# Window mixing on one core: 64-row transposes in two banks, and normalisation moved to GpSimd

## The reference, cut to what matters

```
x = x + mixing(groupnorm(x), w, b)        # 16 heads of 16 channels, windows of 8 x 8 cells
x = x + attention(groupnorm(x), ...)      # projections, depthwise conv, linear attention

def mixing(x, w, b):                      # w: [16, 64, 64], b: [16, 64]
    pad by 4 on every side, cut into 9 x 9 windows of 64 cells
    y[n, head, i, d] = sum_j w[head, i, j] * xw[n, head, j, d] + b[head, i]
    put the windows back, cut the padding off
```

## Time and profile before

| | |
|---|---|
| Median of 3 runs | 2488.25 us (2484.59 to 2489.66) |
| The profiled execution | 2490.49 us, of which its span is 2488.8 us |
| Busy share of the span | PE 95%, PEld 76%, DVE 80%, ACT 60%, POOL 44% |
| Mixing stage, first and last records | image load at 0.8 us, last add to the image at 259.3 us |

### The profile page before, as it was taken

One profiled execution on the slowest core, in us unless ns is written; L12 is line 12 of the kernel. 1 busy time (PEld: TensorE's weight loads), 2 busy tenths in 40 slices (PEclk: granted clock), 3 DMA queues, 4 the chain that ended last, 5 costly groups with the idle time before them and its releaser, 6 DMA issues. The chain is left out here.

```text
span 2488.8 us, 66780 instructions
## 1 busy us (share of the span) xinstructions
PE 2364.8 (95%) x25485; PEld 1886.2 (76%) x25485; DVE 1992.4 (80%) x2652; ACT 1495.8 (60%) x1864; POOL 1099.0 (44%) x1477
## 2 busy tenths in 40 slices
PE   5999799999999999799999999999999889999998
PEld 5889687777787788577888888888888656666666
DVE  7887588787688786788888888888888578888775
ACT  5777576665566566566677677667767433443342
POOL 6722387787787787300000000000000068888887
PEclk9999899999999999899999999999999999999999
DMA  7874688988889889988888888888888677777774
GB/s 283 342 293 177 212 301 313 325 294 306 307 281 323 320 282 321 267 204 204 206 213 208 208 208 210 207 207 212 210 206 209 215 251 271 279 278 271 270 271 135
DMA packets 300877, 628.38 MB, mean 252 GB/s; under 512 B 50688, under 2 KB 252160, under 8 KB 291456
## 3 DMA queue, kind: packets, MB, share of 16 engines
q1 hardware_dynamic: 295616, 590.90, 77.1%
q10 hardware_dynamic: 4048, 31.11, 3.5%
q0 software_dynamic: 1008, 3.67, 0.4%
HBM read 327.81 MB, written 300.94 MB: 253 GB/s over the span
## 5 line engine op out<-in xcount | busy, mean ns | idle before, releaser
L1901 POOL TENSOR_TENSOR ql<-image,qh 128x1024 fp32r<-128x1024 f32 x128 | 305.3, 2410 | 971.4 <-ACT qh L1929 971.4
L1555 PE MATMUL c_ps<-dh,wh 128*128 128x512 f32 x1152 | 463.5, 402 | 17.5 <-DVE wl L1706 13.1
L1470 ACT ACTIVATE dh<-image 128x1632 fp32r<-128x1632 f32 x192 | 301.5, 1570 | 266.7 <-PE c_ps L1555 250.6
L1555 PE MATMUL c_ps<-dh,wl 128*128 128x512 f32 x1152 | 455.0, 395 | 0.0
L1555 PE MATMUL c_ps<-dl,wh 128*128 128x512 f32 x1152 | 453.6, 394 | 1.3 <-issue 1.3
L1664 DVE TENSOR_TENSOR dl<-image,dh 128x1632 fp32r<-128x1632 f32 x192 | 356.4, 1856 | 72.2 <-ACT dh L1470 72.2
L1125 PE MATMUL o_ps<-xh,wqh 128*128 128x512 f32 x768 | 320.8, 418 | 11.0 <-issue 7.6
L1125 PE MATMUL o_ps<-xl,wqh 128*128 128x512 f32 x768 | 304.6, 397 | 0.0
L1125 PE MATMUL o_ps<-xh,wql 128*128 128x512 f32 x768 | 303.4, 395 | 0.0
L1555 PEld LDWEIGHTS c_ps<-dh,wh 128*128 128x128 f32 x1152 | 217.7, 189 | 70.1 <-DVE wl L1706 13.2
L1555 PEld LDWEIGHTS c_ps<-dl,wh 128*128 128x128 f32 x1152 | 217.3, 189 | 53.4 <-issue 1.3
(11 more groups left out here) (210 smaller groups left out, 5024.0 us busy)
## 6 DMA issues: line engine op xcount, KB each, us to landing
qkv_scratch<-stage SPq DMA_DIRECT2D x384, 408.0 KB, 4.0
image<-qkv_scratch SPq DMA_DIRECT2D x189, 816.0 KB, 6.3
qr_scratch<-qs SPq DMA_DIRECT2D x128, 256.0 KB, 3.0
yq_scratch<-qy SPq DMA_DIRECT2D x64, 512.0 KB, 6.7
image<-qr_scratch SPq DMA_DIRECT2D x128, 256.0 KB, 6.2
image<-yq_scratch SPq DMA_DIRECT2D x128, 256.0 KB, 5.9
ox<-x_scratch SPq DMA_DIRECT2D x8, 4096.0 KB, 14.8
out<-ox SPq DMA_DIRECT2D x7, 4096.0 KB, 12.7
```

The costliest lines, as they stand in the source:

```text
L1470: act.activation(dh[kind][:, :], raw[kind], ACT.Copy).then_inc(hi_ready, 1)
L1555: last = pe.matmul(c_ps[:, m, :], w[hp][:, kind, part, o:o + P], cells[:, :, HALF * dy:HALF * dy + HALF * NB], start=(k == 0), stop=(k == 5))
L1901: pool.tensor_tensor(two_of(ql, n, tp), two(n, tp), two_of(qh, n, tp).bitcast(F32), ALU.subtract)\
```

## The change

Five things are edited.

1. A turn has 16 transposes in place of 8: each takes 64 partitions (one array tile of 64 rows and 128 columns) with the 64 x 64 corner of the identity moving through it. The two row halves `ch` alternate, and each has a bank of the pair to itself. `xT` is laid out accordingly as [half of the channels of a tile, window pair and ct, 64 channels].
2. Turning back likewise has 16 transposes of 64 rows; the half v goes to bank v of the pair, and the cells are written in image order.
3. `add_back` adds a bank at a time, 2 operations of 512 elements for even n, and 448, 64, 448, 64 for odd n, in place of 1,024, and 768, 128, 128.
4. The exchange of window rows of tile ct = 1 moves from normalisation to `turn_back` (`halves[v ^ ct]`), so that "inner" is one piece of 1,792 elements per ct and the two border sides are one piece of 256.
5. ACT normalises pieces of image 0 only; from image 1 on POOL does all four pieces of a half. The waits on `xn_ready` stay at 2 from there.

`BY_DVE` is the same in both: DVE has two of eight result banks before and after. The mixing products have the same sizes and count; the products cut in four are now those with row = 1 in place of row != half.

```diff
-        xT = sb("xT", [P, GP, C])
+        xT = sb("xT", [P, 2, GP * CT, HC])
...
             if what == "inner":
-                src = src[:, :, SHIFT:W - SHIFT].rearrange("p r (s c) -> p s r c", c=WS)
-                dst = dst[:, 0:WINS - 1, :, :]
-                if ct == 1:
-                    src, dst = src[:, :, WS * w:WS * w + WS, :], dst[:, :, WS * (w ^ 1):WS * (w ^ 1) + WS, :]
+                src, dst = src[:, :, SHIFT:W - SHIFT].rearrange("p r (s c) -> p s r c", c=WS), dst[:, 0:WINS - 1, :, :]
...
+        PARTS = [(0, "inner"), (1, "inner"), (0, "edges"), (1, "edges")]
 
         def act_parts(b, g):
-            return [(0, "inner", 0)] + [(1, "inner", w) for w in range(rows_by_act(b, g))]
+            return PARTS[0:2 - g] if b == 0 else []
 
         def pool_parts(b, g):
-            return [(1, "inner", w) for w in range(rows_by_act(b, g), WR)] + EDGES
+            return [p for p in PARTS if p not in act_parts(b, g)]
...
                     for ct in range(CT):
-                        o = (a % 2) * C + ct * P
-                        last = pe.transpose(ps[:, pair(f) + a // 2, o:o + P],
-                                            xn[:, ct, column, row:row + 2 * WS, :].rearrange("p r c -> p (r c)"),
-                                            K["ident"][:, :])
+                        o = (CT * a + ct) * HC
+                        for ch in range(2):
+                            last = pe.transpose(ps[:, pair(f) + ch, o:o + HC],
+                                                xn[halves[ch], ct, column, row:row + 2 * WS, :].rearrange("p r c -> p (r c)"),
+                                                K["ident"][halves[ch], halves[ch]])
...
                 for a in range(8):
-                    last = pe.transpose(ps[:, 4 + 2 * (n % 2) + a // 4, P * (a % 4):P * (a % 4) + P],
-                                        yT[:, a0 + a, P * ct:P * ct + P], K["ident"][:, :])
+                    for v in range(2):
+                        cells = ps[:, 4 + 2 * (n % 2) + v, :].rearrange("p (t r s c) -> p t r s c", t=2, r=WS, c=WS)[:, a % 2, :, a // 2, :]
+                        rows = halves[v ^ ct]
+                        last = pe.transpose(cells, yT[rows, a0 + a, P * ct:P * ct + P], K["ident"][rows, rows])
...
+                for v in range(2):
+                    mid = img[:, v, :, :, x0:x0 + inner]
+                    last = dve.tensor_tensor(mid, mid, back[:, v, :, :, 0:inner], ALU.add)
+                    if inner < W // 2:
+                        edge = img[:, v, :, :, 0:W // 2 - inner]
+                        last = dve.tensor_tensor(edge, edge, back[:, v, :, :, inner:W // 2], ALU.add)
```

More of the change, by code:

```diff
@@ L364, in _, with part @@
                     load(b + 3, GR * g, GR * g + GR, x_loaded[(b + 3) % 2][g])
-        def part(op, b, g, ct, what, w):
+        def part(op, b, g, ct, what):
             src, sc, nb = rows_of(b, ct)[:, GR * g:GR * g + GR, :], T["sc"][:, ct:ct + 1], T["nb"][:, ct:ct + 1]
@@ L372, in part @@
             if what == "inner":
[L373 to L382 removed]
+                src, dst = src[:, :, SHIFT:W - SHIFT].rearrange("p r (s c) -> p s r c", c=WS), dst[:, 0:WINS - 1, :, :]
+            else:
+                src = src.rearrange("p r (k c) -> p k r c", c=SHIFT)[:, ::1 - W // SHIFT, :, :]
+                dst = dst[:, WINS - 1, :, :].rearrange("p r (k c) -> p k r c", c=SHIFT)
             return op(dst, src, sc, nb)
[L385 to L388 removed]
+        PARTS = [(0, "inner"), (1, "inner"), (0, "edges"), (1, "edges")]
         def act_parts(b, g):
[L391 removed]
+            return PARTS[0:2 - g] if b == 0 else []
         def pool_parts(b, g):
[L394 removed]
+            return [p for p in PARTS if p not in act_parts(b, g)]
         @block.gpsimd
@@ L423, in normal_slots @@
                 at_least(pool, t_full, N_T * (GROUPS * (b - 1) + g + 1))
-                for ct, what, w in pool_parts(b, g):
-                    last = part(normal, b, g, ct, what, w)
+                for ct, what in pool_parts(b, g):
+                    last = part(normal, b, g, ct, what)
                 last.then_inc(edge_ready, 1)
@@ L451, in normal_slots @@
                 at_least(act, t_full, N_T * (GROUPS * (b - 1) + g + 1))
-                for ct, what, w in act_parts(b, g):
-                    last = part(normal, b, g, ct, what, w)
+                for ct, what in act_parts(b, g):
+                    last = part(normal, b, g, ct, what)
                 last.then_inc(xn_ready, 1)
@@ L459, in fill @@
                 act.wait_ge(t_full, N_T * s + f + 1)
-                act.activation(xT[:, 4 * f:4 * f + 4, :].rearrange("p a c -> p (a c)"),
-                               ps[:, pair(f):pair(f) + 2, :].rearrange("p a n -> p (a n)"), ACT.Copy).then_inc(t_taken, 1)
+                act.activation(xT[:, :, 8 * f:8 * f + 8, :].rearrange("p r a c -> p r (a c)"), ps[:, pair(f):pair(f) + 2, :],
+                               ACT.Copy).then_inc(t_taken, 1)
             def add_bias(s, k, half):
@@ L498, in _ @@
         def _(pe):
-            halves = (slice(0, WS * WS), slice(WS * WS, P))
             def links(b):
@@ L551, in mix @@
                                     .rearrange("p (s t c) -> p s t c", t=2, c=MIX_CH)
-                                cells = xT[halves[row], :, MIX_CH * h:MIX_CH * h + MIX_CH]\
-                                    .rearrange("p (s t) c -> p s t c", t=2)
+                                per, c0 = HC // MIX_CH, MIX_CH * (h % (HC // MIX_CH))
+                                cells = xT[halves[row], h // per % 2, :, c0:c0 + MIX_CH]\
+                                    .rearrange("p (s t k) c -> p s t k c", t=2, k=CT)[:, :, :, half, :]
                                 weights = wT[halves[row], :, (h - row) % MIX_HEADS, :]
-                                whole = 1 if g == GROUPS - 1 and row != half else 2
+                                whole = 1 if g == GROUPS - 1 and row == 1 else 2
                                 for cut_y, ts in ((0, slice(0, whole)), (1, slice(whole, 2))):
@@ L692, in add_back @@
                 bank = 4 + 2 * (n % 2)
-                back = ps[:, bank:bank + 2, :].rearrange("p q n -> p (q n)").rearrange("p (s r c) -> p r s c", s=4, c=WS)
-                img = rows_of(b, ct)[:, GR * g:GR * g + GR, :]
-                inner = 4 - n % 2
-                c0 = SHIFT + 4 * WS * (n % 2)
-                mid = img[:, :, c0:c0 + WS * inner].rearrange("p r (s c) -> p r s c", c=WS)
-                last = dve.tensor_tensor(mid, mid, back[:, :, 0:inner, :], ALU.add)
-                if inner < 4:
-                    for c, y in ((0, W - SHIFT), (SHIFT, 0)):
-                        edge = img[:, :, y:y + SHIFT]
-                        last = dve.tensor_tensor(edge, edge, back[:, :, inner, c:c + SHIFT], ALU.add)
+                back = ps[:, bank:bank + 2, :].rearrange("p v (t r x) -> p v t r x", t=2, x=W // 2)
+                img = rows_of(b, ct)[:, GR * g:GR * g + GR, :].rearrange("p (t v r) x -> p v t r x", t=2, v=2)
+                x0 = SHIFT + W // 2 * (n % 2)
+                inner = min(W // 2, W - x0)
+                for v in range(2):
[4 more added lines that the diff above has]
+                        last = dve.tensor_tensor(edge, edge, back[:, v, :, :, inner:W // 2], ALU.add)
                 last.then_inc(k_taken, 1)
```

18 lines of the change are left out of this document (5 added, 13 removed).

## The result

The changed kernel takes 2496.1 us (median of 12 runs, 2493.2 to 2501.6) beside 2489.6 us of the kernel before (12 runs, 2484.6 to 2491.8), a ratio of 1.003 with a 95% interval of 1.002 to 1.0039. It is 6.6 us slower; 6.2 us less had been forecast, and 2496.1 lies above the range. The profiled execution took 2497.2 us, of which 2495.4 are its span.

A forecast was written before the change was run, and what follows sets the result against it. A closed path through DVE's work, PE's mix, ACT's biases and three transpose batches was taken to set the period; -1.18 (batches) +0.40 (adds) = -0.78 us an image, x 8 = -6.2, to 2482.0; range 2474 to just over 2491.5.

The forecast's parts named there:

- The path: Mixing stage: closed chain of DVE's work, PE's mix, ACT's biases and three transpose batches sets the image period; -0.78 us each.
- the bracket of the reciprocal: DVE's idle time before it goes on with the scale, 1.73 us, was to become near 1.4.
- DVE's bracket ahead of its adds: DVE's wait for turn-back batch 0 before adding, 2.59 us, was to become near 1.6.
- Halving the other 13 batches only makes PE idle.: The 13 of an image's 16 transpose batches that lie beside other work were to give no gain when shortened.
- clock still 1.00 there: Sign of being right: PE's granted clock in the mixing stage stays at the upper level, 2.4 GHz.
- the brackets ahead of back 3 unchanged: PE's wait for DVE before turn-back batch 3 was to stay at 0.76 us.
- Opening and close are of the same kind and inside the 8.: The stage's start and end were to gain like the rest, counted within 8 images at -0.78 us each.
- The late loads: Rival, 4%: the 0.6 us margin of image loads is used up, DVE waits, up to half the gain goes: -3, 2485.
- The slow rivals: Two rivals in the mixing stage, load-bound transposes (5%) and POOL held up by DVE (7%), both left out of the range.
- load-bound transposes: Rival, 5%: each 64-row transpose on PE costs 0.111 us, PE alone sets the period: +93 us, 2581.
- POOL held up by DVE: Rival, 7%: POOL's normalising pieces take 2.4 times as long, a half 11.6 us against 10.2 available: +37 us, 2525.
- All later stages equal: Sign of being right: everything after the mixing stage takes the same time as before.

The follow-up runs named there:

- e10: Changed kernel plus stores and loads split by channel tile, plus two filler products on PE (512 and 384 columns) before turn back 2 and 3: 2482.6 us, ratio 0.9971.
- e5: Changed kernel without the mixing stage's loads of images 3 to 7 (result differs from the reference): 2495.4 us, ratio 1.0021.
- e7: Changed kernel without the loads of images 3 to 7, plus filler products of 512 and 384 columns before turn back 2 and 3: 2485.2 us, ratio 0.9983.
- e12: Changed kernel plus only the two filler products (512 columns before turn back 2, 384 before turn back 3): 2490.7 us, ratio 1.0008.
- e13: Control: the kernel before plus the same two filler products (512 and 384 columns): 2496.1 us, ratio 1.0026.
- e11: Changed kernel with every batch of transposes issued twice into the same places: 2534.2 us, ratio 1.018.
- e2: Kernel before with only the 64-row back turns and the adds a bank at a time: 2490.3 us, ratio 1.0005.
- e3: Kernel before with only normalisation moved, all of it on POOL from image 1 on, in the old layout: 2495.6 us, ratio 1.0027.
- e8: Changed kernel with each half image stored and loaded as two channel tiles, the first once its first two adds are done: 2492.0 us, ratio 1.0006.
- e9: Kernel before with each half image stored and loaded as two channel tiles: 2487.2 us, ratio 0.999.
- e4: Changed kernel plus small filler products of 128 columns, three before turn back 2 and two before turn back 3: 2493.6 us, ratio 1.0018.

## Why the prediction was wrong

- **The path and most of its terms held.** Batches of 0.66 to 0.71 (forecast 0.70), POOL's pieces to 0.01 us, the bracket of the reciprocal at 1.36 (1.4), DVE's bracket ahead of its adds at 1.78 (1.6), and periods of 27.76 in after and 27.70 and 27.71 in e10 (27.7). The adds of 512 and 64 elements came as 0.679 and 0.213. On the rule of the Trainium skill ("TensorE: Matmul & The Clock Gate", LDWEIGHTS), 107 ns for each load of 128 columns: 32 in a row take 1.22 here, of which the last is 0.27, so (1.22 - 0.27) / 31 = 0.031 each (0.0284 forecast); the measurement decides against the rule taken alone, for two row groups in turn.
- **The step that failed: "Halving the other 13 batches only makes PE idle."** The forecast gave that idleness no price and kept the clock at 1.00, "clock still 1.00 there". It also had "the brackets ahead of back 3 unchanged", where 0.76 became 1.21. PE's busy time went from 26.24 to 21.49 of 28.45, the gap ahead of back 2 from nothing to 1.64, and PE was granted the lower clock for 34 us of the stage, which made four mixes 4.1 us longer. e5, e7, e10, e12 and the control e13 show it: with the gaps filled the mixes are back at 6.0 to 6.3 where no issue wait cuts them and e10 has the forecast period, and without gaps to fill the fillers only cost.
- **A term that was missing: PE's own instructions.** 16 short transposes in place of 8 need more instructions in less time. 6.1 us of issue waits stand in after, 22.0 in e11, 0.2 before, and they end 2.2 to 2.9 us after a packet of the instruction queue. The forecast counted matmuls by their durations and never by their number.
- **A term that was sized wrong: "Opening and close are of the same kind and inside the 8."** The mix of the second image starts at 61.63 before, at 63.49 in after and still at 62.75 in e10, so the first image loses 1.1 us even there. PE waits 1.8 (e10 1.5) for DVE's first biases ahead of the scale chain, which starts at 39.10 (e10 39.29) and not at 38.20. From the second image on e10's stage is 5.0 shorter than before's; with the 1.1 that makes its 3.8.
- **The late loads** had 4% and -3 us. They came (1.2 us in 2 waits), and e2 shows a late load of 0.79 growing through a lower clock. They were a smaller part: without loads e5's median is only 0.7 us under after's.
- **The size.** The stage was to shorten by 6.2 us and lengthened by 6.3. Of these 12.5, 4.1 are the four slow mixes, 6.1 the issue waits and 1.2 the loads, 11.4 together, and the opening is about 1 more. Not all of an issue wait lies on the path, slow transposes aren't in it, and one of the slow mixes is in the opening, so this is an order of size and not a balance.
- **The slow rivals** (load-bound transposes, POOL held up by DVE) didn't occur. The lock of a shared port that the Trainium skill describes ("SBUF — State Buffer", Terms) left no mark: 1.836 us for pieces of 1,792 is the line of POOL's short pieces.
- **All later stages equal** held: 2221.6 and 2221.9 from the first product on.

What stays open: why e10 is 7 us faster in the medians while its stage is 3.8 us shorter in the profile. Its later stages take 2217.7, and those of e3, e7, e8 and e12 2217.3 to 2217.4, in one execution each; those of e5 take 2225.8, the others' 2220.2 to 2221.9. Nothing there was changed. Compared with e9, the kernel before with the same split, e10 is 4.6 us faster, near the 3.8 of the stage and the forecast's 6.2. Also open is the reason why the instruction fetches come in time with split stores and loads; that the transfers compete was not tested apart, and e5, with DMA at 0.36, still has 3.8 us of issue waits. And it is not shown what it takes to keep the clock up: no run varies the gaps alone, and stretches at half clock remain among the transposes even in e10.

## What to carry to other kernels

When a change shortens PE's work off the path, price the emptiness: look for where PE will now wait just ahead of its longest run of products, and forecast that run at the lower clock as a rival of its own (here 7.0 to 8.5 us for 6.3). The same stretch among short work beside the path cost nothing here. If it happens, two products that fit into the gaps can give back more than the change lost; a control in the kernel before tells whether it is the clock that they restore. Where one instruction is replaced by two half as long, compare the number of instructions per us with the rest of the program, and look for cut batches with "issue" in their bracket.

## What the runs showed of the hardware

- Transposes on two 64-row tiles in turn cost 0.031 us each, between 0.014 for four tiles of 32 rows and 0.114 for one of 128. At the lower clock a batch of 16 takes 1.12 in place of 0.71.
- More work on PE did not bring the same clock in every form: e11 has its transposes doubled and still 23.9 us at half clock, together with its issue waits; e4 with five small products 17.1; e12 with two large ones 6.8. The three differ in their gaps too, so which kind of work counts is not shown.
- Removing work from DMA gained nothing (e5, 2495.4 after 2496.1), and in the profiled execution, the slowest of 12, seven of eight images had a mix of 6.97 to 8.45 at a clock partly halved.
- A stretch at half clock that lies among transposes cost nothing in the period (27.76 in the changed kernel, stretch from 72.0 on); in a mix a stretch of 3.4 cost 0.85 to 1.3 us.
- A batch of transposes can stop in its midst for 2.4 us with no semaphore involved; all 13 issue waits of the changed kernel and e12, in batches and in mixes, end 2.2 to 2.9 us after a 16 KB packet of the instruction queue.
